# A convolution scan layer hands one injection in three to GpSimd

## The reference, cut to what matters

```python
def step(h, inp):                      # one place; delta, u: 192 channels, B, C: 16 states
    dt, ut, bt, ct = inp
    h = exp(dt * A) * h + dt * bt * ut     # decay * state + injection
    y = sum_n(h * ct)                      # read
```

## Time and profile before

| | us |
|---|---|
| median of three runs | 3560.6 |
| the profiled execution, its own time | 3562.11 |
| its span, first to last instruction | 3560.3 |
| layer L2, head to tail, about | 1570 to 2130 |
| its four stages (first tile to last read) | 1641 to 2071 |
| VectorE busy, of the span | 2978.8 (84%) |
| GpSimd busy | 2819.5 (79%) |
| TensorE busy | 2462.7 (69%) |
| ScalarE busy | 2042.1 (57%) |

### The profile page before, as it was taken

How to read it: one execution, slowest core, us unless ns; L and a number is a source line. 1 busy time by engine, 2 the same in 40 slices (tenths; PEclk the granted TensorE clock), 3 DMA queues, 4 the chain that set the end, 5 groups by cost and what they waited for, 6 DMA issues and landing times. The chain is left out here.

```text
span 3560.3 us, 27492 instructions
## 1 busy us (share of the span) xinstructions
PE 2462.7 (69%) x5948; PEld 618.4 (17%) x5948; DVE 2978.8 (84%) x1934; ACT 2042.1 (57%) x2262; POOL 2819.5 (79%) x1212
## 2 busy tenths in 40 slices
PE   5777677777677677335677776766777676767676
PEld 2111111111111111111111112111111111111111
DVE  1799999999989898675989841998999898999995
ACT  3566565757566665304655524756675656657573
POOL 0899999999999998003666622999999999999995
PEclk9777786888788877667788778768887888779787
DMA  1656556574755465103442502664737555655654
GB/s 42 159 137 152 133 142 149 126 171 111 178 136 142 121 154 126 30 0 90 122 108 78 122 7 68 148 161 124 170 104 177 136 142 132 154 132 145 150 125 106
DMA packets 140881, 437.19 MB, mean 123 GB/s; under 512 B 33909, under 2 KB 34619, under 8 KB 140395
## 3 DMA queue, kind: packets, MB, share of 16 engines
q1 hardware_dynamic: 140714, 435.58, 51.2%
HBM read 307.56 MB, written 6.82 MB: 88 GB/s over the span
## 5 line engine op out<-in xcount | busy, mean ns | idle before, releaser
L885 POOL TENSOR_TENSOR L_read<-L_state,L_c_rows 128x1024 f32<-128x1024 f32 x768 | 1795.2, 2358 | 79.6 <-DVE L_state L993 76.5
L671 PE MATMUL L_y_ps<-L_read,L_fold 128*64 128x512 f32 x3072 | 1027.8, 765 | 450.0 <-POOL L_read L885 448.1
L818 ACT ACTIVATE L_work_ps<-L_delta,L_a_neg 128x1024 f32<-128x1024 f32 x256 | 286.3, 1118 | 592.4 <-DVE L_state L993 592.3
L872 POOL TENSOR_TENSOR L_state<-L_du,L_b_rows 128x1024 f32<-128x1024 f32 x256 | 603.6, 2358 | 26.9 <-POOL L_read L885 4.2
L993 DVE TENSOR_TENSOR_SCAN L_state<-L_decay,L_work_ps 128x1024 f32<-128x1024 f32 x256 | 585.3, 2286 | 26.7 <-DVE L_work_ps L974 2.5
L993 DVE TENSOR_TENSOR_SCAN L_state<-L_work_ps,L_state 128x1024 f32<-128x1024 f32 x256 | 581.0, 2269 | 22.8 <-POOL L_state L872 21.8
L818 ACT ACTIVATE L_decay<-L_delta,L_a_neg 128x1024 f32<-128x1024 f32 x512 | 584.3, 1141 | 15.1 <-DVE L_state L993 10.1
L993 DVE TENSOR_TENSOR_SCAN L_state<-L_decay,L_row_ps 128x1024 f32<-128x1024 f32 x256 | 585.4, 2287 | 8.8
L974 DVE TENSOR_TENSOR L_work_ps<-L_du,L_row_ps 128x1024 f32<-128x1024 f32 x256 | 314.3, 1228 | 200.2 <-issue 147.0
L671 PEld LDWEIGHTS L_y_ps<-L_read,L_fold 128*64 128x64 f32 x3072 | 182.6, 157 | 1201.6 <-POOL L_read L885 912.2
L1523 POOL TENSOR_TENSOR L_read<-L_state,L_c_rows 128x1024 f32<-128x1024 f32 x96 | 237.7, 2476 | 164.8 <-DVE L_state L1629 140.0
(11 more groups left out here) (324 smaller groups left out, 2896.4 us busy)
## 6 DMA issues: line engine op xcount, KB each, us to landing
L_b_rows<-L_bc_dram SPq DMA_DIRECT2D x580, 256.0 KB, 4.2
L_c_rows<-L_bc_dram SPq DMA_DIRECT2D x580, 256.0 KB, 4.1
L_delta<-L_delta SPq DMA_DIRECT2D x204, 256.0 KB, 6.0
L_du<-L_du SPq DMA_DIRECT2D x140, 256.0 KB, 6.2
L_du<-L_u SPq DMA_DIRECT2D x64, 256.0 KB, 6.1
L_bc_dram<-L_dbl SPq DMA_DIRECT2D x40, 128.0 KB, 3.5
L_delta<-L_delta_a SPq DMA_DIRECT2D x16, 256.0 KB, 4.4
L_du<-L_du_a SPq DMA_DIRECT2D x16, 256.0 KB, 5.0
```

Source lines behind the costliest of these rows:

```text
L671: m = nc.tensor.matmul(y_to(c, o, i), fold[:, :], y_half(t, o, i), start=first, stop=last, skip_group_check=True)
L818: nc.scalar.activation(to[:, :], delta2[:, d * NBLK + c, :], ACT.Exp, scale=a_neg[:, o * 2 + d, c, p:p + 1]).then_inc(decay_ready, 1)
L872: nc.gpsimd.tensor_tensor(state[:, last, :], du2[:, d * NBLK + last, :], b_rows[:, g % 2, :], ALU.mult).then_inc(injected_c, 1)
L885: nc.gpsimd.tensor_tensor(read[:, t % READS, :], state[:, t % STATES, :], c_rows[:, g % 2, :], ALU.mult).then_inc(multiplied, 1)
```

## The change

Of the three injections of a group, VectorE keeps c = 0 and c = 1. That of c = 2 is formed by GpSimd, straight into `state[:, 2]`, from a row of B in SBUF; the scan of c = 2 then runs in place. The decay of c = 2 goes to PSUM (`work_ps`), so that this scan too has one operand in PSUM. `b_rows` has two places, and the two `b_ps` become `row_ps` (the row) and `work_ps` (c = 0's injection, then c = 2's decay). Layers L0, L1 and L3 stay as they are, and so do the tables of side work.

```diff
-        decay = sb("decay", [128, DECAYS, L])
+        decay = sb("decay", [128, DECAYS - 1, L])
-        b_rows = sb("b_rows", [128, L])
+        b_rows = sb("b_rows", [128, 2, L])
-        b_ps = [ctx.enter_context(nc.psum_tensor(f"{name}_b_ps{i}", [128, L], F32)) for i in range(2)]
+        row_ps = ctx.enter_context(nc.psum_tensor(f"{name}_row_ps", [128, L], F32))
+        work_ps = ctx.enter_context(nc.psum_tensor(f"{name}_work_ps", [128, L], F32))
...
+        MULT0, SCAN0, SUM0, INJECT0, READY0 = NBLK + 1, DECAYS, READS, 1, 2
...
             def load_b(image, g):
                 G = image * NP + g
                 sp.wait_ge(b_ready, G + 1)
+                sp.wait_ge(injected_c, G + 1)
                 for h in range(2):
                     row = g + NP * h
-                    sp.dma_start(b_rows[quarter(h), :],
-                                 bc_dram[image, row:row + 1, :].to_broadcast([BLK, L])).then_inc(b_in, 16)
+                    sp.dma_start(b_rows[quarter(h), G % 2, :],
+                                 bc_dram[image, row:row + 1, :].to_broadcast([BLK, L])).then_inc(b_in[G % 2], 16)
...
             def copy_b(G):
-                act.wait_ge(b_in, 32 * (G + 1))
+                act.wait_ge(b_in[G % 2], 32 * (G // 2 + 1))
                 if G > 0:
                     act.wait_ge(scanned, (G - 1) * NBLK + 2 + SCAN0)
-                nc.scalar.copy(b_ps[G % 2][:, :], b_rows[:, :]).then_inc(b_ready, 1)
+                nc.scalar.copy(row_ps[:, :], b_rows[:, G % 2, :]).then_inc(b_ready, 1)
...
                     act.wait_ge(scanned, number * NT + t - DECAYS + 1 + SCAN0)
-                    nc.scalar.activation(decay[:, t % DECAYS, :], delta2[:, slot(number, c), :], ACT.Exp,
+                    if c == 2:
+
+                        act.wait_ge(scanned, number * NT + t - 1 + SCAN0)
+                    to = work_ps if c == 2 else decay[:, c, :]
+                    nc.scalar.activation(to[:, :], delta2[:, slot(number, c), :], ACT.Exp,
                                          scale=a_neg[:, c, p:p + 1]).then_inc(decay_ready, 1)
...
+            def inject_c(number, p):
+
+                G, last = number * NP + p, NBLK - 1
+                if p == 0:
+                    pool.wait_ge(du2_in[last], (number + 1) * per_block[last])
+                pool.wait_ge(b_in[G % 2], 32 * (G // 2 + 1))
+                pool.wait_ge(multiplied, G * NBLK + MULT0)
+                nc.gpsimd.tensor_tensor(state[:, last, :], du2[:, slot(number, last), :], b_rows[:, G % 2, :],
+                                        ALU.mult).then_inc(injected_c, 1)
...
                 for t, (p, c) in enumerate(tiles):
+                    if c == 0:
+                        inject_c(number, p)
                     pool.wait_ge(scanned, number * NT + t + 1 + SCAN0)
...
                 if c == 0:
-                    dve.wait_ge(b_ready, G + 2)
-                to = row if c == 2 else b_ps[1 - G % 2]
-                if c < 2:
+                    dve.wait_ge(b_ready, G + 1 + READY0)
                     dve.wait_ge(scanned, T + SCAN0)
-                nc.vector.tensor_tensor(to[:, :], du2[:, slot(number, c), :], row[:, :], ALU.mult).then_inc(injected, 1)
+                to = row_ps if c == 1 else work_ps
+                nc.vector.tensor_tensor(to[:, :], du2[:, slot(number, c), :], row_ps[:, :], ALU.mult).then_inc(injected, 1)
+                dve.wait_ge(injected, G * 2 + c + 1 + INJECT0)
...
-                    fed = inject_tile(number, t)
-                    dve.wait_ge(injected, T + 1 + INJECT0)
+                    if c < 2:
+                        by, fed = decay[:, c, :], inject_tile(number, t)
+                    else:
+                        by, fed = work_ps, state[:, c, :]
+                        dve.wait_ge(injected_c, number * NP + p + 1 + READY0)
                     dve.wait_ge(decay_ready, T + 1)
                     dve.wait_ge(multiplied, T - STATES + 1 + MULT0)
-                    nc.vector.tensor_tensor_scan(state[:, t % STATES, :], decay[:, t % DECAYS, :], fed[:, :], 0.0,
-                                                 ALU.mult, ALU.add).then_inc(scanned, 1)
+                    nc.vector.tensor_tensor_scan(state[:, c, :], by[:, :], fed[:, :], 0.0, ALU.mult,
+                                                 ALU.add).then_inc(scanned, 1)
```

More of the change, by code:

```diff
@@ L1123, in conv_scan_layer @@
         c_rows = sb("c_rows", [128, 2, L])
-        b_rows = sb("b_rows", [128, L])
+        b_rows = sb("b_rows", [128, 2, L])
         bc_dram = nc.dram_tensor(f"{name}_bc_dram", [B, 2 * NS, L], F32, kind="Internal").ap()
         y_ps = ctx.enter_context(nc.psum_tensor(f"{name}_y_ps", [128, 3, HALF], F32))
-        b_ps = [ctx.enter_context(nc.psum_tensor(f"{name}_b_ps{i}", [128, L], F32)) for i in range(2)]
+        row_ps = ctx.enter_context(nc.psum_tensor(f"{name}_row_ps", [128, L], F32))
+        work_ps = ctx.enter_context(nc.psum_tensor(f"{name}_work_ps", [128, L], F32))
         side_ps = ctx.enter_context(nc.psum_tensor(f"{name}_side_ps", [128, HALF], F32))
         (set_up, consts, side_ready, side_free, conved_s, u_ready, sp_abs, sp_exp, sp_log, sp_one,
-         sp_less, sp_gap, sp_relu, sp_du, decay_ready, scanned, injected, b_ready,
-         multiplied, y_added, bc_stored, b_in, y_free, y_out, rooted, silued, gated, x_added) = (
+         sp_less, sp_gap, sp_relu, sp_du, decay_ready, scanned, injected, injected_c, b_ready,
+         multiplied, y_added, bc_stored, y_free, y_out, rooted, silued, gated, x_added) = (
             sem(s) for s in (
@@ L1136, in conv_scan_layer @@
                 "sp_exp", "sp_log", "sp_one", "sp_less", "sp_gap", "sp_relu", "sp_du", "decay_ready",
-                "scanned", "injected", "b_ready", "multiplied", "y_added", "bc_stored", "b_in", "y_free", "y_out", "rooted",
+                "scanned", "injected", "injected_c", "b_ready", "multiplied", "y_added", "bc_stored", "y_free", "y_out",
+                "rooted",
                 "silued", "gated", "x_added"))
@@ L1141, in conv_scan_layer @@
         c_in = [sem(f"c_in{d}") for d in range(2)]
+        b_in = [sem(f"b_in{d}") for d in range(2)]
         per_block = (16 * 2, 16 * 2, 16 * 4)
-        MULT0, SCAN0, SUM0, INJECT0 = NBLK + 1, DECAYS, READS, 1
+        MULT0, SCAN0, SUM0, INJECT0, READY0 = NBLK + 1, DECAYS, READS, 1, 2
         def wait_side(eng, n):
@@ L1178, in copy_block @@
                 if was >= 0:
-                    sp.wait_ge(injected, was * NT + NT - NBLK + last + 1 + INJECT0)
+                    if last < NBLK - 1:
+                        sp.wait_ge(injected, (was * NP + NP - 1) * 2 + last + 1 + INJECT0)
+                    else:
+                        sp.wait_ge(injected_c, (was + 1) * NP + READY0)
                 copy_rows(du2, du, image, q, du2_in[q])
@@ L1333, in _ @@
                 side(tail, key, i)
-                keep_busy(b_ps[0][:, 0:HALF], FILL_AFTER.get((key, i), FILL))
+                keep_busy(row_ps[:, 0:HALF], FILL_AFTER.get((key, i), FILL))
         @block.scalar
@@ L1535, in _ @@
             for s, n in ((scanned, SCAN0), (multiplied, MULT0), (y_added, SUM0), (injected, INJECT0), (side_free, 1),
-                         (y_free, 1), (x_added, 1), (b_ready, 1)):
+                         (y_free, 1), (x_added, 1), (b_ready, READY0), (injected_c, READY0)):
                 for _ in range(n):
@@ L1598, in inject_tile @@
                 G = number * NP + p
-                row = b_ps[G % 2]
                 if p == 0:
```

## The result

The changed kernel takes 3588.5 us (median of six runs, 3578.5 to 3599.4), the kernel before 3560.4 on the same chip (six runs, 3556.7 to 3570.2): ratio 1.007, 95% interval 1.0052 to 1.0089. It is slower, by 28 us where I forecast 20.9. The profiled execution took 3599.4, the longest of the six; its time is 37 above that of before, and 10.9 above its own median, so sizes read from it are more likely too large than too small.

What follows compares the result with a forecast made beforehand. VectorE was taken as the fullest engine in every stage, with ScalarE lacking slack at tile 11. Terms 1.8 + 7.7 + 3.9 + 5.6 + 3.3 + 5.6 - 7.0 = +20.9 on 3560.6 gave 3581.5 us, range 3550 to 3596.

Steps and rivals of the forecast that it cites:

- ScalarE at tile 11: Stages 1 and 2: decay waits one scan more, its chain starts 4.6 us later, injection 15 comes +5.6 us in each.
- Stage 0, read 20: Stage 0 from scan 8: late softplus and GpSimd's added injections make read 20 end +7.7 us later.
- the race: Tap 0 against GpSimd's read 3 at a stage's start: read issues 0.2 us earlier; a tap win saves 2.0 to 2.4 each.
- Start and taps: Start of stages: GpSimd's injection 0 awaits the du copy, taps collide with reads; +1.8, +3.9, +3.3 us in stages 0, 1, 2.
- Free groups: Groups of three tiles held by nothing else: from 10.68 to about 9.4 us, a gain of 1.3 each.
- Stage 3: -7.0: Stage 3, without preparation or taps: VectorE's saved injections make it 7.0 us shorter, between -4 and -10.
- the bound of -4: Smallest gain given for stage 3, in us, if the side chain binds again.
- From injection 15 to injection 21 I take 0.: Stages 1 and 2: the chain of side results, not VectorE, sets this 28.45 us stretch, so no change.
- second: Losses halved: taps go ahead of reads, stage 0's late read 15 is partly regained; +10 us, 3571; chance 0.18.
- third rivals: GpSimd piles up, behind at every pair of taps in stages 0 to 2: +42 us, 3602; chance 0.07.
- the first: Meant gain comes: ScalarE loses under about 1 us at tile 11, VectorE gains 30 us, 3531; chance 0.17.

Runs made afterwards that it cites:

- short fill: Changed kernel plus zero-weight TensorE matmuls in stages 0 to 2, 10 ahead of tile 7's y product and 18 ahead of "bc": 3584.3 us, ratio 1.0061.
- g3_fill: Changed kernel with 20 zero-weight matmuls meant ahead of "bc" in stages 0 to 2; the trace shows none, so it is the changed kernel again: ratio 1.0053.
- e1_wait_only: Kernel before, with only ScalarE's wait for one scan more ahead of the decay of c = 2 tiles; nothing moved to GpSimd: 3588.0 us, ratio 1.0066.
- g2_no_pool_injection: Changed kernel without GpSimd's injection product; its scan takes the C row instead, all waits kept: 3584.5 us, ratio 1.0054.
- long fill: Changed kernel plus zero-weight TensorE matmuls in stages 0 to 2, 16 ahead of tile 7's y product and 32 ahead of "bc": 3593.8 us, ratio 1.0089.
- filled kernel before: Kernel before plus zero-weight TensorE matmuls in stages 0 to 2, 12 ahead of tile 7's y product and 20 ahead of "bc": ratio 1.0022.

## Why the forecast held, and where it was off

The sign, the range (3550 to 3596) and the main place were right. The single sizes were less so: in the profiled execution, from read 20 to read 20, the four stages came out at +6.3, +17.7, +10.7 and +1.7 (stage 3 to the end of its last scan), where 9.5, 9.5, 8.9 and -7.0 were forecast. By the steps of the prediction:

- **ScalarE at tile 11.** Injection 12 forecast 16.4 after the last tap, measured 16.66 in stages 1 and 2; in stage 0 15.2 and 15.19. Injection 15 forecast 31.6: 31.72 in stage 2, but 35.84 in stage 1. The wait is shown as the cause of this shift by the run that has it alone.
- **Stage 0, read 20.** Forecast 7.7 + 1.8 late, measured 6.3. From the end of scan 8 to read 20 it was 7.5, as forecast. But scan 8 ended 1.3 earlier than before, and not 1.8 later: the tap won the race there (tap 0 took 0.73 us, though tap 1 then took 3.27).
- **Start and taps.** Forecast +3.9 and +3.3, measured +3.4 and +4.1, and the taps collide as described: in stage 1 tap 0 took 2.93 us. GpSimd's product alone gave the kernel before +3.4 and +3.9.
- **Free groups.** One group of stage 3 takes 2044.25 - 2034.97 = 9.28 us, as forecast (9.3 to 9.4).
- **The step that failed: "Stage 3: -7.0".** By the same measure, from read 20 to the end of the last scan, it came out at +1.7. Scan 8 was forecast to end 39.7 after read 20 and ended at 44.4. GpSimd's injection 0 waits for du of block 2, which let it start 17.9 after read 20 and not 16.2. Read 0 stands behind it, and so TensorE has nothing to do:

```profile
2021.08 1.97 PE L1326 MATMUL L_y_ps<-L_read,L_fold 128*64 128x512 f32 x4 [9.47 <-POOL L_read L1546]
...
2027.10 2.07 PE L1305 MATMUL L_side_ps<-g_cm,L_w_z 96*128 96x512 f32 x2
...
2033.70 1.23 DVE L1628 TENSOR_TENSOR L_work_ps<-L_du,L_row_ps 128x1024 f32<-128x1024 f32 x1 [3.34 <-ACT L_row_ps L1450]
...
2016.29 2.34 POOL L1532 TENSOR_TENSOR L_state<-L_du,L_b_rows 128x1024 f32<-128x1024 f32 x1 [3.52 <-DMA L_du<-L_du_b]
```

These are TensorE, VectorE and, last, GpSimd's injection 0, of the changed kernel: after 9.47 us of idle time the gate's matmuls run at the lower level, the gate's results reach ScalarE late, and the copy of the B row stands behind them: 3.34 us of waiting at tile 6. In the run with the short fill the same places read:

```profile
2007.47 1.98 PE L1335 MATMUL L_y_ps<-L_read,L_fold 128*64 128x512 f32 x4 [7.32 <-POOL L_read L1555]
...
2012.55 1.12 PE L1310 MATMUL L_side_ps<-g_cm,L_w_z 96*128 96x512 f32 x2
...
2017.25 1.23 DVE L1638 TENSOR_TENSOR L_work_ps<-L_du,L_row_ps 128x1024 f32<-128x1024 f32 x1 [0.49 <-ACT L_row_ps L1459]
...
2002.68 2.35 POOL L1541 TENSOR_TENSOR L_state<-L_du,L_b_rows 128x1024 f32<-128x1024 f32 x1 [2.26 <-DMA L_du<-L_du_b]
```

No fill stands in stage 3. There the clock has recovered by 2012 and tile 6 waits 0.49. Scan 8 ends 2026.43 - 1986.06 = 40.4 us after read 20, against the 39.7 forecast, and the stage is 3.6 shorter than before, just outside the bound of -4 that I gave. So of the 8.7 us by which this term was off, 2.9 at tile 6 go with the clock, which the prediction priced at nothing anywhere. Another 1.3 are du's copy, which came that much earlier in the second execution. Some 1.3 more arose behind scan 8 and I have not traced them, and the last 3.4 are missing in both executions. In g3_fill, a further execution of the same work, the stage was 2.7 shorter than before. So -7.0 was too much in all three.
- **"From injection 15 to injection 21 I take 0."** It was 28.45 and became 32.95 in stage 1 and 29.32 in stage 2. With the 4.2 us at the "shift" sums, stage 1 (read 20 to read 20) came out at +17.7 where 9.5 was forecast; stage 2 at +10.7 against 8.9. What failed is that I took TensorE's durations after the stall from the trace of before. Where they come out at the lower level, they set VectorE's pace. It came out so in stage 1 of this execution and of e1_wait_only, in both stages of g3_fill (31.5 and more), and in stage 2 of this execution it did not.

**The account of the layer,** from the table: the wait alone +28.0 (of it 13.1 the stall at tile 12 in three stages and 10.0 in tiles 12 to 18 of stages 1 and 2), VectorE's saved injections -15.2 (e1_wait_only to g2_no_pool_injection), GpSimd's product +23.8 (from there to the changed kernel). These add up to the 36.6 between the two sums, but the last two sizes are not to be relied on: the changed kernel's profiled execution lies 10.9 us above its median and that of g2_no_pool_injection 5.0 below. In the ratios (1.0066, 1.0054, 1.0070) these two steps are smaller, about 4 and 6 us, and cancel each other within the intervals. GpSimd's product alone, in the kernel before, cost about 10 us (1.0027). The second and third rivals (3571, 3602) lie outside what all six runs of the changed kernel show; of the first, the condition (under half of 4.6 us late) was plainly not met.

**Left open:** why the clock falls in one stage of an execution and not in the next, whether the fill or chance held it in the changed kernel, and what the change would gain with both the wait and the SBUF operand gone. That needs a third decay in PSUM, whose place is taken, and was not tried.

## What to carry to other kernels

When an operation moves to another buffer, look at what that buffer's earlier use makes its writer wait for, and walk everything queued behind that writer: here one wait on ScalarE, 4.6 us deep at one tile of a stage, took back more than the 32 saved injections brought. Work moved to an engine with spare time still costs where it meets the giver with both reading SBUF, so price it at the collisions and not by busy shares. And a stall of one engine is not only its own length: the profile of before gives TensorE's durations for one execution of its own idle gaps, and the same work can take twice as long elsewhere.

## What the runs showed of the hardware

- A scan with both operands in SBUF took 3381 ns on average with GpSimd reading SBUF beside it, 2275 ns with the decay in PSUM, and 2287 with the decay in SBUF and the injection in PSUM. With both in SBUF and no GpSimd operation beside it, it took 2.28 us.
- TensorE's "shift" matmuls took 2.02 us at the lower level and 1.08 at the upper. In stage 1 of the changed kernel the level came back 7 us after the 11.79 us gap (1.08 at 1822.03) and had fallen once more by 1829, with waits of only 0.7 and 1.5 us in between. In the run with the long fill it held at 1.00 from 1796 to 1853, through the same short waits. In the filled kernel before it fell at 1930 after a wait of 2.61 us, from 1.00 to 0.57.
- Executions of one kernel on one chip spread over 17 us for the kernel before (3557.7 to 3574.6, 19 runs), wider than the three runs at the outset (3560.1 to 3570.2). The profiled executions differ in which stage's tiles 12 to 18 run slowly: 35.5 and 27.8 us in stages 1 and 2 of the changed kernel's, 33.3 and 31.5 in g3_fill's, which has the same work.
